# Edge sums of two graph attention layers: 512 columns in one bank, five items in flight, and the tail columns summed apart

## The reference, cut to what matters

```python
h = (x @ W).reshape(n, heads, out_ch)
al_s = jnp.einsum('nhc,hc->nh', h, a_src)
al_d = jnp.einsum('nhc,hc->nh', h, a_dst)
e = jax.nn.leaky_relu(al_s[src] + al_d[dst], 0.2)
emax = jax.ops.segment_max(e, dst, num_segments=n)
ee = jnp.exp(e - emax[dst])
denom = jax.ops.segment_sum(ee, dst, num_segments=n)
alpha = ee / (denom[dst] + 1e-16)
out = jax.ops.segment_sum(h[src] * alpha[:, :, None], dst, num_segments=n)
```

## Time and profile before

| what | value |
|---|---|
| device time, median of 3 | 4422.83 us (4421.45 to 4423.59) |
| profiled execution: span of the core | 4980.9 us |
| profiled execution: mean granted TensorE clock | 0.851 |
| busy share PE, DVE, ACT, POOL | 73%, 56%, 40%, 41% |
| items of GAT layer 1 (first sum to last add) | 1872 to 2548 us |
| items of GAT layer 2 | 2790 to 3469 us |
| adds of GAT layer 3 | 3709 to 4319 us |

### The profile page before, as it was taken

How to read it: one execution, slowest core, us unless ns; L and a number is a source line. 1 busy time by engine, 2 the same in 40 slices (tenths; PEclk the granted TensorE clock), 3 DMA queues, 4 the chain that set the end, 5 groups by cost and what they waited for, 6 DMA issues and landing times. The chain is left out here.

```text
span 4980.9 us, 76392 instructions
## 1 busy us (share of the span) xinstructions
PE 3649.6 (73%) x19614; PEld 2886.2 (58%) x19615; DVE 2794.6 (56%) x8633; ACT 2014.6 (40%) x6637; POOL 2027.2 (41%) x2092
## 2 busy tenths in 40 slices
PE   6677777795999457778778678776726665667995
PEld 3455555585888346666545566665624444456885
DVE  4567676646122457776666677765726555773112
ACT  0466666421222137668633567665310100021221
POOL 0566665000222025666611466663066666202221
PEclk9788887896999769999988799998856676778998
DMA  2566666354778657776633677664344443304556
GB/s 77 180 185 183 188 181 178 93 151 105 259 266 279 229 212 224 213 222 204 180 114 138 205 214 242 207 178 137 118 154 146 140 127 106 93 27 155 190 179 222
DMA packets 353521, 859.19 MB, mean 172 GB/s; under 512 B 52389, under 2 KB 162828, under 8 KB 344588
## 3 DMA queue, kind: packets, MB, share of 16 engines
q0 software_dynamic: 144384, 455.22, 30.5%
q1 hardware_dynamic: 208780, 399.80, 24.3%
HBM read 770.02 MB, written 84.81 MB: 172 GB/s over the span
## 5 line engine op out<-in xcount | busy, mean ns | idle before, releaser
L1866 POOL DMA_INDIRECT h<-h_table,src_of x944 | 907.2, 961 | 1050.0 <-PE ps L1900 505.5
L1880 PE MATMUL ps<-h,gat_layer_hot 128*128 128x261 f32 (+1 forms) x3136 | 896.6, 436 | 302.0 <-issue 93.3
L1880 PEld LDWEIGHTS ps<-h,gat_layer_hot 128*128 128x128 f32 x3136 | 636.9, 213 | 475.8 <-issue 260.4
L745 POOL DMA_INDIRECT edges_rows<-kv_table,src_of x464 | 462.0, 996 | 402.5 <-DVE edges_out_rows L844 150.6
L2138 DVE TENSOR_TENSOR acc<-acc,ps 128x522 f32 (+1 forms) x696 | 418.0, 601 | 308.9 <-PE ps L1880 168.2
L1965 ACT ACTIVATE h<-h,gat_shared 128x128 f32<-128x128 f32 x1872 | 581.1, 390 | 4.6 <-issue 2.5
L1866 POOL DMA_INDIRECT x<-h_table,src_of x448 | 429.8, 959 | 227.9 <-issue 111.5
L1880 PE MATMUL ps<-x,gat_layer_hot 128*128 128x261 f32 (+1 forms) x1504 | 425.5, 432 | 114.2 <-DVE x L2115 47.0
L1032 ACT ACTIVATE acc<-ps,moe_experts_b 128x256 f32<-128x256 f32 (+1 forms) x512 | 200.5, 443 | 614.2 <-PE ps L982 590.7
L1880 PEld LDWEIGHTS ps<-x,gat_layer_hot 128*128 128x128 f32 x1504 | 303.2, 211 | 195.2 <-issue 95.1
L982 PE MATMUL ps<-moe_experts_turned,moe_experts_w 128*128 128x256 f32 (+1 forms) x2048 | 403.3, 355 | 5.0 <-DMA moe_experts_w<-in_L_ffn_W 5.0
(11 more groups left out here) (377 smaller groups left out, 5693.7 us busy)
## 6 DMA issues: line engine op xcount, KB each, us to landing
moe_experts_w<-in_L_ffn_W SPq DMA_DIRECT2D x128, 1024.0 KB
gat_layer_hots<-hot_table SPq DMA_DIRECT2D x174, 562.0 KB
hot_table<-acc SPq DMA_DIRECT2D x58, 562.0 KB
h<-h_table,src_of POOLq DMA_INDIRECT x944
edges_dst_row<-dst_rows SPq DMA_DIRECT2D x58, 256.0 KB
acc<-src_rows SPq DMA_DIRECT2D x58, 256.0 KB
acc<-dst_rows SPq DMA_DIRECT2D x58, 256.0 KB
h_table<-h SPq DMA_DIRECT2D x10, 1280.0 KB
```

The source lines that it names most:

```text
L745: nc.gpsimd.indirect_dma_start(rows[:, r, s, :], None, k.kv_table, bass.IndirectOffsetOnAxis(ap=k.src_of[:, 2 * t + s:2 * t + s + 1], axis ...
L1866: nc.gpsimd.indirect_dma_start(g.rows(t, e, 0, W), None, g.table, bass.IndirectOffsetOnAxis(ap=k.src_of[:, 2 * t + e:2 * t + e + 1], axis= ...
L1880: mm = nc.tensor.matmul(k.ps[t % S * PIECES + p][:, 0:PIECE], hot[:, t % HOTS, e, :], g.rows(t, e, p * PIECE, (p + 1) * PIECE), start=(e = ...
```

## The change

`PIECES` goes. In layers 1 and 2 `sum_item` multiplies 512 columns (`MAIN`) in one bank, with two matmuls. `S` becomes 5, `LAG` 4. The nine tail columns (`TAIL`) are not copied behind the rows any more, and ACT's copy goes. `tail_of_item`, new on PE, multiplies them straight from `g.sums`, four items after the item's main sum (`BEHIND`), and accumulates them over a chunk of 64 items in bank 5, at the columns of the item's node tile. It reads the tile's number into a register of PE. At a chunk's start a matmul of zeros opens the accumulation. DVE's new `drain` adds the 25 x 9 columns of the bank to `acc` once per chunk. `weigh` waits for `tails` in place of `summed`, for a place of `hot`. Layer 3 keeps its form (`APART` is false).

```diff
-    PIECES = 2 if FULL > 512 else 1
-    PIECE = -(-FULL // PIECES)
+    TAIL, APART = g.tail, g.own_tail
+    MAIN = W if APART else FULL
     HOTS, NB = 12, 4
-    S = 6 // PIECES
+    S = 5 if APART else 6
     LAG = S - 1
+    BEHIND = LAG
...
-                for p in range(PIECES):
-                    for e in range(2):
-                        mm = nc.tensor.matmul(k.ps[t % S * PIECES + p][:, 0:PIECE], hot[:, t % HOTS, e, :],
-                                              g.rows(t, e, p * PIECE, (p + 1) * PIECE), start=(e == 0), stop=(e == 1))
+                for e in range(2):
+                    mm = nc.tensor.matmul(k.ps[t % S][:, 0:MAIN], hot[:, t % HOTS, e, :],
+                                          g.rows(t, e, 0, MAIN), start=(e == 0), stop=(e == 1))
                 mm.then_inc(summed, 1)
+
+            def tail_of_item(t):
+                if t % CH == 0:
+                    pe.wait_ge(emptied, t // CH + 1)
+                    pe.wait_ge(tailed, t // CH + 1)
+                    nc.tensor.matmul(k.ps[5][:, 0:TILES * TAIL], void[0:1, 0:P], void[0:1, P:P + TILES * TAIL], start=True, stop=False)
+                ends_here = t % CH == CH - 1 or t == ITEMS - 1
+                n = pe.value_load(k.item_tile[0:1, t:t + 1], min_val=0, max_val=TILES - 1)
+                for e in range(2):
+                    mm = nc.tensor.matmul(row(tail_bank, n, 0, TAIL), hot[:, t % HOTS, e, :], sums(t)[:, e, :],
+                                          start=False, stop=ends_here and e == 1)
+                mm.then_inc(tails, 1)
...
                 if t >= 0:
                     sum_item(t)
+                if APART and t >= BEHIND:
+                    tail_of_item(t - BEHIND)
                 q = scored(t)
                 if q is not None:
                     products(q)
+            if APART:
+                for t in range(ITEMS - BEHIND, ITEMS):
+                    tail_of_item(t)
...
-                last = act.copy(g.rows(t, slice(None), W, FULL), sums(t))
+                if not APART:
+                    last = act.copy(g.rows(t, slice(None), W, FULL), sums(t))
...
                 if t >= HOTS:
-                    dve.wait_ge(summed, t - HOTS + 1)
+                    dve.wait_ge(tails if APART else summed, t - HOTS + 1)
...
+            def drain(c):
+
+                here = k.acc[:, :, W:FULL]
+                dve.wait_ge(tails, min(c * CH, ITEMS))
+                v.tensor_tensor(here, here, tail_bank, ALU.add).then_inc(emptied, 1)
+                dve.wait_ge(emptied, c + 1)
...
                 elif t % CH == 0:
+                    if APART:
+                        drain(t // CH)
                     rescale(t // CH)
...
-                acc = k.acc[:, bass.ds(n, 1), 0:PIECES * PIECE].rearrange("p a (q c) -> p (a q) c", q=PIECES)
-                v.tensor_tensor(acc, acc, k.psum[:, t % S * PIECES:t % S * PIECES + PIECES, 0:PIECE], ALU.add).then_inc(added, 1)
+                acc = row(k.acc, n, 0, MAIN)
+                v.tensor_tensor(acc, acc, k.ps[t % S][:, 0:MAIN], ALU.add).then_inc(added, 1)
```

More of the change, by code:

```diff
@@ L1732, in __init__ @@
         self.first_hot = room[:, 3 * SUBP:3 * SUBP + P]
-        self.pitch = -(-self.full // 4) * 4
+        self.own_tail = self.full > 512
+        self.pitch = self.W if self.own_tail else -(-self.full // 4) * 4
         self.rings = [(room, n, room[:].rearrange("p t w -> p (t w)")[:, 0:n * 2 * self.pitch].rearrange("p (r s w) -> p r s w", s=2, w=self.pitch))
@@ L1825, in phase_gat_layer @@
         nought = ph.sb("nought", [P, 1])
+        void = ph.sb("void", [1, P + TILES * TAIL])
         picked, rest = g.picked, g.rest
@@ L1837, in phase_gat_layer @@
             ph.sem(n) for n in ("marked", "weighed", "scaled", "summed", "added", "cleared", "noughts", "padded"))
+        emptied, tails = ph.sem("emptied"), ph.sem("tails")
         block = ph.block()
         bank = k.ps[6:8]
+        tail_bank = k.ps[5][:, 0:TILES * TAIL].rearrange("p (t w) -> p t w", w=TAIL)
         wide_bank = k.ps[6][:, 0:H * E].rearrange("p (h e) -> p h e", h=H)
@@ L1972, in softmax @@
                         act.wait_ge(weighed, (c - 1) * CH)
+                        if APART:
+                            act.wait_ge(tails, (c - 1) * CH)
                     act.activation(g.sums[:, c % 2, :, 0:H], back.rearrange("p h s -> p s h"), ACT.Exp).then_inc(exped, 1)
@@ L1984, in _ @@
                     act.wait_ge(noughts, 1)
-                    act.copy(k.acc[:, :, 0:PIECES * PIECE], nought[:].rearrange("p (t a) -> p t a", t=1).to_broadcast([P, TILES, PIECES * PIECE])
+                    act.copy(k.acc[:, :, 0:FULL], nought[:].rearrange("p (t a) -> p t a", t=1).to_broadcast([P, TILES, FULL])
                              ).then_inc(cleared, 1)
@@ L2067, in softmax @@
                         dve.wait_ge(scaled, (c - 1) * CH)
+                        if APART:
+                            dve.wait_ge(tails, (c - 1) * CH)
                     last = k.is_last[:, cols].rearrange("p (a s) -> p a s", a=1)
@@ L2095, in softmax @@
                     dve.sem_inc(factored, 1)
+            if APART:
+                v.memset(void[:], 0.0).then_inc(emptied, 1)
             if g.pitch > FULL:
@@ L2150, in _ @@
                     softmax(c, n)
+            if APART:
+                drain(CHUNKS)
 def phase_gat_nodes(k, g):
```

## The result

The changed kernel takes 4483.43 us (median of 4 executions, 4481.79 to 4484.09) against 4422.14 us. The ratio is 1.0134 [1.0122, 1.0146], 61 us slower.

What follows compares the result with a forecast made beforehand. POOL's gathers were taken as the bound, 547 us a layer; after the change PE's 535 + 15 + 3 + 4 = 557, the difference raised to 20 a layer, 40 for both: 4422.8 + 40 = 4463 us, range 4385 to 4570.

Steps and rivals of the forecast that it cites:

- The bound before: Layers 1 and 2 before the change: POOL's gathers set the pace, 2.54 us an item, 547 us a layer.
- Main sum on PE: PE's wide matmuls per item: 1.76 us before, 1.72 after, a gain of 0.04.
- Softmax stretches: Three stretches of some 22 items a layer, where DVE is slower than PE: 5 us each, 15 us.
- Chunk starts: PE waits for DVE's drain before opening the next chunk's tails: 1 us for each of three a layer.
- Two engines of nearly the same need lose more than either alone, so I take 20: POOL and PE in layers 1 and 2: the difference of 10 us a layer raised to 20, 40 for both.
- Register load: Tile number read on PE: hidden behind the main sum, 0 us an item, bounds 0 and 0.85.
- Last tails and drain: Layer's end: four tails stand alone, about 0.9 us each, 4 us; DVE's drain add takes less than 0.70 us.
- More in flight, ACT's copy, DVE's add: Layers 1 and 2: five sums in flight, ACT's 0.09 us copy gone, one-bank add 0.01 us shorter; nothing booked.
- B: Rival: DVE's adds hold layers 1 and 2, so the deeper lag gains 33 us each: 4357 us; chance 0.25.
- C: Rival: PE is already the bound in layers 1 and 2, so every added 0.32 us counts: 4585 us; chance 0.11.
- D: Rival: PE's register load isn't hidden, up to 394 us more, 4860 us; chance 0.04.
- A: Rival: late, bunched sum signals stay as traced in layers 1 and 2; 4430 or 4446 us; chance 0.18.

Runs made afterwards that it cites:

- the second profile: The kernel before, unchanged, profiled again at the 4420 us pace; 4420.78 us.
- the padded kernel before: The kernel before with two idle 9-column matmuls (four passes) ahead of each item's sum in layers 1 and 2; 4486.19 us, ratio 1.0136.

## Why the prediction was right, and where its sizes were off

**The sign and the case.** The forecast was that the tails bring PE to its limit, slower, 4463 us with 4433 to 4503 for this case alone. Measured 4483.43. The mechanism is shown from four sides: PE at 98% in the changed layers; no tails, no loss; the same passes in the old kernel, a loss of the same size; and half of the gathers helps the old kernel alone. What the prediction had wrong are sizes: the main sum's (19 us a layer too little) and, in its own words, "1 us for each of three chunk starts" (11 us a layer too little).

**The bound before.** POOL at 2.54 us an item: 2.52 in the second profile. The prediction's 547 us for a layer were 554. That the waits of the earlier trace rows would be small without whatever made the profile long was an assumption, and it held; but the prediction put the 558 us to the profiled execution. They go with the chip: on the long one the kernel takes as much in all 13 executions, and the second profile's span is 4419.0 us.

**Main sum on PE, the first mis-sized term.** The prediction took 1.72 us from the earlier trace rows and a gain of 0.04. It takes 1.80. The four passes of the earlier trace rows stand behind two passes of 128 columns (L608), as the next group does; this is the first profile:

```profile
1737.72 0.41 PE L608 MATMUL ps<-ident,gat_shared 128*128 128x128 f32 x2
1737.97 1.88 PE L620 MATMUL ps<-gat_w,gat_shared 128*128 128x512 f32 x4
1739.69 0.51 PE L620 MATMUL ps<-gat_wa,gat_shared 128*128 128x8 f32 x4
```

In the changed kernel the sum stands behind passes of 9 or 24 columns, and there its first pass takes 0.51 us start to start (1904.70 to 1905.22), each other one 0.43. Over layers 1 and 2 the first pass has a median of 0.51 us behind products and tails, and of 0.43 in the 14 items where a 128-column pass of the softmax stands before it. So what counts is the width of the pass before: behind a short one the first pass is 0.08 us longer. Why is not shown; that its weights can't be loaded beside so short a pass would fit. 232 x 0.08 = 19 us a layer. The kernel before pays the same, but only behind products: there its sum takes 1.84 us (1901.39 to 1903.23 in the timeline below), 1.80 on the mean of two sums in a row.

```profile
1901.39 2.01 PE L1880 MATMUL ps<-x,gat_layer_hot 128*128 128x261 f32 x8
1903.23 0.69 PE L1897 MATMUL ps<-gat_layer_parts,gat_layer_hots 128*128 128x100 bf16 x12
...
1906.34 3.77 PE L1880 MATMUL ps<-x,gat_layer_hot 128*128 128x261 f32 x16
1909.94 0.69 PE L1897 MATMUL ps<-gat_layer_parts,gat_layer_hots 128*128 128x100 bf16 x12
```

**Tail on PE.** 0.36 us, as taken from the eight-column row.

**Softmax stretches.** The prediction booked 5 us for each of three. In them DVE holds PE now and then, as it said. Timeline of PE in the changed kernel:

```profile
1855.26 1.95 PE L1884 MATMUL ps<-h,gat_layer_hot 128*128 128x512 f32 x4
...
1858.14 1.95 PE L1884 MATMUL ps<-h,gat_layer_hot 128*128 128x512 f32 x4 [0.57 <-DVE gat_layer_hot L2136]
...
1860.68 1.95 PE L1884 MATMUL ps<-h,gat_layer_hot 128*128 128x512 f32 x4 [0.24 <-issue]
```

These items start 2.88 and 2.54 us apart, where PE's own work is 2.16. Over a whole stretch it is less: the sums of items 43 to 64 start 2.31 us apart, and the three stretches of layer 1 hold 3.2 + 3.5 + 3.4 = 10 us more than 2.16 us an item, in place of 15. PE's own softmax matmuls are part of it.

**Chunk starts, the second mis-sized term.** The prediction booked 1 us for each of three, since "PE has by then the main sum of the same item to do". DVE's side of it, at the start of the second chunk of layer 1, and PE's:

```profile
1879.08 0.56 DVE L2143 TENSOR_SCALAR x<-x,gat_shared 128x128 f32<-128x128 f32 x2
1882.46 0.39 DVE L2150 TENSOR_TENSOR acc<-acc,ps 128x225 f32<-128x225 f32 x1 [2.82 <-PE ps L1896]
1885.60 0.69 DVE L2175 TENSOR_TENSOR acc<-acc,ps 128x512 f32 x1 [0.86 <-DVE acc L2160]
1887.72 0.62 DVE L2143 TENSOR_SCALAR x<-x,gat_shared 128x128 f32<-128x128 f32 x2
...
1882.28 1.96 PE L1884 MATMUL ps<-x,gat_layer_hot 128*128 128x512 f32 x4
1888.44 3.75 PE L1884 MATMUL ps<-x,gat_layer_hot 128*128 128x512 f32 x4 [2.45 <-DVE x L2143]
1893.80 2.32 PE L1884 MATMUL ps<-x,gat_layer_hot 128*128 128x512 f32 x4
```

DVE stands still for 2.82 us, as `drain` waits for the chunk's last tails, which PE does four items behind. With the drain and `rescale` behind it, no rows are scaled from 1879.64 to 1887.72, and then PE waits 2.45 us for them. It waits 2.21 and 1.79 us at the other two chunk starts of the layer. Behind the first of these gaps the granted clock was 0.50 (1888 to 1894), the level of 1.2 GHz, and the main sum took 3.54 us (1888.44 to 1891.98). Counted by the starts of PE's sums, less 2.16 us an item and 0.63 with products, the three chunk starts of layer 1 cost 6.3 + 3.2 + 4.4 = 14 us in place of 3; layer 2's cost 14 as well. In the padded kernel before, which has `rescale` but no `drain`, PE has no gap there. So about 14 of a layer's 581 us come from a wait that the change brought, not from passes. What a kernel with the tails and without this wait would take was not run.

**The sum again.** 232 x 2.16 = 501, 84 x 0.63 = 53, softmax stretches 10, chunk starts 14 and some 3.5 in the first items, which start at a low clock (0.53 from 1708 to 1714), make 581, where the trace has 580.3 and 581.3 to the end of the last main sum. The prediction had 535 + 15 + 3 = 553 up to there: 19 too little in the main sum, 11 in the chunk starts, 3.5 in the first items, and 5 too much in the softmax stretches. Against 554 before, a layer loses 26, and 2 more with the last tails.

**"Two engines of nearly the same need lose more than either alone, so I take 20".** The number came close to the measured 28 by luck, and its reason fails: the changed kernel with half of the gathers gains 4.5 to 7 us in all, so POOL and PE hardly disturb each other. Plain sizes that were too small, by 25 us after the change (557 against 582, with the last tails) and by 7 before, made up for it.

**Register load.** Hidden, as predicted; its 0.30 us on PE's queue equals the row on DVE. The Trainium skill's floor of about 600 ns ("DMA: Bandwidth & Descriptors", latency and other measured facts) is twice what was measured.

**Last tails and drain.** Each of the four was booked at 0.9 us, on the thought that the load and its register instructions would show there. Twenty passes follow in one row, 2.30 us long, so the four cost some 0.45 us each, under 2 us together: the loads are issued ahead. The drain itself takes 0.39 us, eight times; what costs is DVE's wait for the tails before it, 24.7 us in all, which at six of the eight is a chunk start as above.

**More in flight, ACT's copy, DVE's add.** All booked at nothing or nearly so: together 1.0004 without the tails, where POOL is the bound and would hide a small gain.

**The rivals.** B rested on waits of 130 us a layer that were the long chip's: 11.7 us of DVE's waits for sums are left in the second profile. C was wrong on the stage, though PE was nearer to its bound than the 461 us in the prediction: the cover was 46 us a layer, not 543 - 461 = 82. D falls. A describes the long chip; its +3.5 to +11.5 us a layer, 4430 to 4446, wasn't measured, since only a variant was timed there (tails behind the products: 10.5 and 16 us a layer more, 0.7% in all).

## What to carry to other kernels

Splitting a matmul into a wide and a narrow part cost whole passes with weights of their own: four passes of nine columns took 0.36 us and slowed the wide pass behind them by 0.08, while the nine columns had cost 0.04 us inside two equal pieces. Before putting work on an engine that isn't the bound, measure its cover: take work from the bound engine and see how far the time falls; here half of the gathers gave 46 us a layer, and the change spent 72. Take a duration from a row with the same neighbours: the first 512-column pass took 0.51 us behind passes of 9 or 24 columns, and 0.43 behind passes of 128. And follow a new wait to the end: DVE's wait for the last tails looked covered, but it delayed what DVE makes for PE next.

## What the runs showed of the hardware that was not expected

The same program takes 4420 us on some chips and 4980 on others. On the long kind the granted clock is lower on average (0.851 against 0.897), but in the layers' stretches it is 0.95 against 0.99, which is too little for 676 us against 555. PE's busy time there, 535.89 against 501.45 us, holds 34 of the 121 us; the rest are waits for PE's sums, on DVE 89.8 us against 11.7 by the same name, and the sums are seen late and in bunches. In the run with half of the gathers and no tails DVE's wait for sums is 6.7 us, and a layer takes 501 us, while layer 3 with all of its gathers stays long. So they go with POOL's full stream of indirect gathers; why the sums are seen late on this kind of chip alone is open, and wasn't settled by any run here.

The stream of indirect gathers in the second profile is very regular: 1.26 us each, 0.95 us of it busy on POOL and 0.30 us to the next.
